# Cross-attention and FP8 feed-forward on one core: pair 2's statistics moved ahead, batch 0's residual moved into stage 1, weight casts regrouped

## The chip, the cores and the metric

One core of one Trainium2 chip runs the whole kernel in one launch. The metric is device time in microseconds (us), lower is better, as the median of the runs. Engines are PE (TensorE), DVE (VectorE), ACT (ScalarE), POOL (GpSimd) and SP, which here only issues DMAs.

## The reference

```python
x = x + xattn(layernorm(x), ctx, ctx, Wq, Wk, Wv, Wfc, bfc)   # 16 batches x 128 tokens x 512, fp32
#   q = x Wq.T (32 heads of 16); k, v = ctx Wk.T, ctx Wv.T (8 groups of 16, 4 heads share one)
#   softmax(q k.T / 4) v, then Wfc and its bias
x = x + ffn(layernorm(x))                # operands rounded to float8_e4m3
#   gelu(x Wg0) * (x Wg1), hidden 2048, then W_linear back to 512
```

## The kernel before, in words

The 16 batches go in 8 pairs (`NB = 2`). Stage p computes the attention of pair p in slots n = 0 to 18 (`SLOTS`; DVE has one more), and in the same slots prepares pair q = p + 1: its layer norm, keys (k), values (v), transposed x (x), queries (q) and the first score tiles for the row maxima. Behind the slots of stages 1 to 7 come units: a unit is a quarter of one batch's gate and ff products (32 matmuls of 128 columns), which ACT evicts (`gate_out`, `ff_out`) and DVE multiplies and rounds to fp8 (`product`, `act_fp8`). Stage 0 has no units, stage 1 has twelve (batches 0, 1 and 2), later ones eight. The second FFN product (`down`) lies in the slots of the next stage.

The order on each engine is written by hand: all five engine programs walk the same slots and units, and `PLAN_0`, `PLAN_1` and `PLAN` say in which slot a step lies. Engines run their own program in order and meet only at semaphores, so a step in a bad slot holds up all that stands behind it on its engine.

In a slot PE does `scores_t` (L618, the transposed scores of one head group), `weigh_values` (L639, L641) of the tile three slots back, and what the plan adds: `scores` (L587, for the maxima), `project_k`, `project_v` (L541), `turn_x` (L552), `project_q` and `project_out` (L506 to L508), `turn_out` (L655), `turn_x2` (L689). ACT exponentiates twice (`weights`: L921, L924), POOL forms the low part (`weights_lo`, L1412) that `weigh_values` needs, and DVE forms the maxima (`maxima`, L1182), the sums and quotients of the outputs (L1193, L1195, L1205) and the low parts of split fp32 operands (L1091, `keys_lo` L1157). The layer norm is `norm_stats` (L1112 to L1117, DVE), a power on POOL (`norm_rstd`, L1386), a copy of the root into a PSUM bank (`roots_1`, L1128) and `norm_apply_psum` (L1141, DVE). A batch's chain behind attention is `turn_out`, `out_hi`, `out_lo`, `project_out`, `residual` (L1219 to L1225), `norm2_rstd` (L1391), `roots_2`, `norm2_apply_psum` (L1241), `turn_x2`, `x2_out` (L936).

The FFN weights come as fp32 chunks of 128 x 1024 into staging places that are used in turn. POOL clamps a chunk (`chunk_clamp`, L1432), ACT casts it (`chunk_cast`, L862), and SP loads the next chunk for the place behind that cast; five chunks go over DVE instead (`chunk`, L1105). SP's queue also issues the DMAs that stack keys, queries and maxima (`mask_k`, `stack_k`, `stack_q`, `stack_max`) in one fixed order.

PSUM has eight banks, A, T, O and G with two each. `bank_sequence` writes down which product takes which bank, and a product waits for the reader of the one ahead of it in its bank. `exp_table` and `gelu_table` load ACT's function tables between attention and FFN.

Of the kernel before, what the change touches and what calls it, by code (L numbers as in the profile page):

```python
# [147 lines left out]
def bank_sequence():  # L148
# [6 lines left out]
    seq += [(("X", 1, 0), "A1"), (("X", 1, 1), "A0"), (("M", 0, 1), "G0"), (("Q", 1, 0), "A1"), (("Q", 1, 1), "A0")]  # L155
    seq += [(("S", 1, 0, s), name) for s, name in enumerate(("G0", "G0", "G0", "G0", "A1", "G0", "A1", "G0"))]
# [23 lines left out]
def xattn_ffn_kernel(nc, x_d, ctx_d, w_d, bfc_d, out_d):  # L180
    ctx = ExitStack()
    with ctx:
# [321 lines left out]
        def _(pe):  # L504
# [153 lines left out]
            def project_out(b, lo, hi):  # L658
                if lo == 0:
# [10 lines left out]
                    if chain_in_e(b) and b and b + 5 <= BATCHES:  # L670
# [109 lines left out]
            for p in range(NP):  # L780
# [3 lines left out]
                for n in range(SLOTS):  # L784
# [9 lines left out]
                    if p == 1 and n == X2_FIRST:  # L794
                        turn_x2(0)
# [25 lines left out]
                for k in range(len(units(p))):  # L821
# [14 lines left out]
                    if q < NP:  # L836
                        for s in BEHIND_UNIT.get(k, ()):
# [12 lines left out]
        def _(act):  # L850
# [168 lines left out]
            for p in range(NP):  # L1019
                q, plan = p + 1, PLANS[p]  # L1020
                chain, c_b = plan["chain"], max(0, NB * p - 1)
                for n in range(SLOTS):
# [8 lines left out]
                    if p == 1 and n == X2_FIRST:  # L1031
# [57 lines left out]
        def _(dve):  # L1089
# [47 lines left out]
            def norm_apply_psum(q, i):  # L1137
# [152 lines left out]
            keys_lo(1)  # L1290
            values_sum(1)
            late = list(W_DVE)
            for p in range(NP):
# [3 lines left out]
                for n in range(SLOTS + 1):  # L1297
# [47 lines left out]
                u0, c_b = units_through(p - 1), NB * p
                for k in range(len(units(p))):
# [190 lines left out]
```

## Time and profile before

| | |
|---|---|
| median of 3 runs | 446.52 us (445.78 to 449.13) |
| the profiled execution | 447.5 us, its span 445.7 us |
| granted PE clock, mean over the span | 0.988 of full speed |
| slots of stage 0 on PE | about 30.4 to 61.0 us |
| slots of stage 1 on PE | 61.0 to about 96.2 us |
| units of stage 1 on PE | about 96.2 to 125.0 us |

The profile is of one execution. Times of rows count from the start of its span, and the time outside the span is 447.5 - 445.7 = 1.8 us. Busy times are of one engine; the idle time of a row stands in brackets, with the instruction that ended it.

### The profile page before, as it was taken

The page shows a single profiled execution, that of the slowest core. Times are in us where ns is not written, and L with a number is a line of the kernel's source. Part 1 is how long each engine was busy: PE and PEld are TensorE (multiplying, and loading weights), DVE is VectorE, ACT ScalarE, POOL GpSimd, SP SyncE. Part 2 cuts the span into 40 slices and gives each one's busy share as a digit, 9 for nine tenths or more (in the row PEclk, how much of TensorE's full clock was granted, in tenths as well). Part 3 has the DMA queues.
Part 4 walks back from the last instruction along what each step waited for, and adds up shares of the span by engine and source line. Part 5 has one row for each costly group of instructions (what it writes and reads, how often), then busy time and mean ns, then how long its engine had stood idle before and what let it go on. Part 6 is the DMA issues. An engine that isn't in the chain of part 4 may idle for free.

```text
span 445.7 us, 11828 instructions
## 1 busy us (share of the span) xinstructions
PE 419.2 (94%) x4620; PEld 342.0 (77%) x4620; DVE 328.5 (74%) x705; ACT 313.4 (70%) x579; POOL 241.5 (54%) x232
## 2 busy tenths in 40 slices
PE   7868878989989999999999999999999999899997
PEld 7756556878866779877987789877887789657983
DVE  3786887588958578975997679975997679576442
ACT  6748849877897645888479755888479755895541
POOL 5388888966447613586228823686328823393000
PEclk9998998999999999999999999999999999999999
DMA  8887981568622551034701552034701342000001
GB/s 297 287 200 256 297 224 37 134 203 246 221 93 67 171 126 46 0 83 133 168 4 38 153 127 68 2 84 134 166 3 32 91 107 63 1 26 26 1 27 47
DMA packets 21287, 50.06 MB, mean 112 GB/s; under 512 B 4688, under 2 KB 5200, under 8 KB 21200
## 3 DMA queue, kind: packets, MB, share of 16 engines
q1 hardware_dynamic: 21054, 48.89, 38.5%
q8 instruction: 37, 0.61, 0.6%
q10 hardware_dynamic: 178, 0.41, 0.4%
q14 instruction: 18, 0.15, 0.1%
HBM read 23.86 MB, written 4.19 MB: 63 GB/s over the span
## 4 chain that ended last, share of the span: by engine, by line
PE 78%; DVE 11%; ACT 5%; issue 3%; DMA 1%; POOL 1%; DVEq 0%; POOLq 0%; ACTq 0%
PE bank L719 21%; PE bank L741 11%; PE bank L506 8%; PE bank L507 7%; PE bank L508 7%; PE bank L618 6%; PE bank L587 6%; DVE mneg L1182 4%; PE bank L639 3%; PE bank L641 3%; PE bank L541 2%; PE bank L552 2%; DMA qs<-mrow 1%; PE bank L655 1%; DVE prod L1247 1%
## 5 line engine op out<-in xcount | busy, mean ns | idle before, releaser
L1412 POOL TENSOR_TENSOR plo<-p,phi 128x512 f16<-128x512 f32 x128 | 148.4, 1170 | 57.1 <-ACT phi L924 56.1
L719 PEld LDWEIGHTS bank<-x2T,wgate 128*128 128x128 fp8e4 x2048 | 115.5, 98 | 11.6 <-issue 8.6
L719 PE MATMUL bank<-x2T,wgate 128*128 128x128 fp8e4 x2048 | 123.7, 219 | 0.8 <-DVE xr L1260 0.5
L921 ACT ACTIVATE p<-bank 128x512 f32<-128x512 f32 x128 | 77.6, 606 | 25.4 <-PE bank L618 24.5
L1182 DVE TENSOR_REDUCE mneg<-bank 128x4 fp32r<-128x512 f32 x128 | 83.9, 684 | 13.4 <-PE bank L587 13.4
L924 ACT ACTIVATE phi<-bank 128x512 f16<-128x512 f32 x128 | 77.3, 604 | 0.0
L741 PE MATMUL bank<-wlin,act 128*128 128x512 fp8e4 x256 | 70.8, 378 | 0.0
L943 ACT ACTIVATE gate<-bank 128x512 bf16<-128x512 f32 x64 | 38.3, 598 | 39.4 <-PE bank L719 38.2
L947 ACT CAST ff<-bank 128x512 bf16<-128x512 f32 x64 | 37.6, 587 | 34.5 <-PE bank L719 34.1
L618 PE MATMUL bank<-qs,ks 98*128 98x512 f32 x128 | 55.7, 435 | 4.3 <-DMA qs<-mrow 3.4
L587 PE MATMUL bank<-kmask,cq 128*128 128x512 f32 x128 | 51.6, 455 | 6.9 <-DVE mneg L1182 4.0
L639 PEld LDWEIGHTS bank<-vt,plo 128*128 128x128 f16 x512 | 31.9, 96 | 24.9 <-issue 21.3
L1391 POOL TENSOR_TENSOR rstd<-var,half_neg 128x1 f32<-128x1 f32 x16 | 8.8, 550 | 77.3 <-DVE var L1225 77.3
L639 PE MATMUL bank<-vt,plo 128*128 128x49 bf16 x512 | 44.8, 187 | 0.8 <-DVE ao L1205 0.8
L1247 DVE TENSOR_TENSOR prod<-gate,ff 128x512 bf16<-128x512 bf16 x64 | 33.7, 527 | 15.3 <-ACT ff L947 15.3
L641 PE MATMUL bank<-vt,phi 128*128 128x49 bf16 x512 | 43.0, 184 | 0.0
L506 PE MATMUL bank<-cx,wq 128*128 128x256 f32 x112 | 39.8, 355 | 1.5 <-DVE cx L1091 1.5
L1396 POOL TENSOR_TENSOR cx<-cin,cx 128x512 fp32r<-128x512 f32 x14 | 17.7, 1273 | 41.7 <-ACT cx L871 41.7
L1195 DVE TENSOR_REDUCE osum<-bank 128x128 f32<-128x384 f32 x64 | 35.7, 557 | 2.2
L1254 DVE TENSOR_SCALAR act<-prod 128x512 fp8e4<-128x512 bf16 x64 | 30.6, 478 | 2.9
L641 PEld LDWEIGHTS bank<-vt,phi 128*128 128x128 f16 x512 | 32.5, 97 | 0.1
L587 PEld LDWEIGHTS bank<-kmask,cq 128*128 128x128 f32 x128 | 22.8, 196 | 12.2 <-DVE mneg L1182 6.7
(112 smaller groups left out, 813.9 us busy)
## 6 DMA issues: line engine op xcount, KB each, us to landing
qs<-cq SPq DMA_DIRECT2D x93, 128.0 KB, 2.4
stage<-in_w SPq DMA_DIRECT2D x22, 512.0 KB, 4.7
ks<-khl SPq DMA_DIRECT2D x96, 64.0 KB, 2.0
cin<-in_ctx SPq DMA_DIRECT2D x8, 512.0 KB, 4.1
xr<-in_x SPq DMA_DIRECT2D x16, 256.0 KB, 4.3
out<-xr SPq DMA_DIRECT2D x16, 256.0 KB, 2.7
kmask<-khl SPq DMA_DIRECT2D x28, 64.0 KB, 2.0
raw<-in_w SPq DMA_DIRECT2D x3, 512.0 KB, 6.3
```

What stands on the lines that cost most here:

```text
L506: pe.matmul(out, a[1], b[0], start=first, stop=False)
L587: pe.matmul(bank_of("S", q, i, s)[:, :], cq[:, 0, j, tok(i)], kmask[:, 2 * half:2 * half + 2, :, tok(i)], start=True, stop=True).then_inc( ...
L618: pe.matmul(T[n % 2][:, :], ks[rows, p % 2, g // 2, g % 2, tok(i)], qs[rows, g // 2, :, tok(i)], start=True, stop=True).then_inc(st_done, 1)
L639: pe.matmul(out, plo[:, (TILES * p + n) % PBUF, j * SEQ:(j + 1) * SEQ], vt[:, p % 2, i, g, :], start=True, stop=False)
L641: mm = pe.matmul(out, phi[:, (TILES * p + n) % PBUF, j * SEQ:(j + 1) * SEQ], vt[:, p % 2, i, g, :], start=False, stop=True)
L719: mm = pe.matmul(out[:, h * SEQ:(h + 1) * SEQ], wgate8[:, UH * v + h, kk, part, :], x2T[:, b % ABUF, kk, :], start=kk == 0, stop=kk == KT - 1)
L741: mm = pe.matmul(lin_bank(b)[:, :], act8[:, b % ABUF, h, :], wlin8[:, h, :], start=h == 0, stop=h == HT - 1)
L921: act.activation(p32[:, e % P32BUF, :], T[n % 2][:, :], ACT.Exp, scale=QUARTER).then_inc(p32_ok, 1)
L924: act.activation(phi[:, e % PBUF, :], T[n % 2][:, :], ACT.Exp, scale=QUARTER).then_inc(phi_ok, 1)
L943: act.activation(gate[:, u % 2, :], up_bank[u % 2][0][:, :], ACT.Gelu_apprx_tanh).then_inc(gelu_ok, 1)
L1182: dve.tensor_reduce(dst[:, :, 2 * half:2 * half + 2, j].rearrange("p a r -> p r a"), bank_of("S", q, i, s)[:, :].rearrange("p (r a k) -> p ...
L1412: pool.tensor_tensor(plo[:, e % PBUF, :], p32[:, e % P32BUF, :], phi[:, e % PBUF, :], ALU.subtract).then_inc(plo_ok, 1)
```

## The change

Slots and units of stages 0 and 1 are rearranged; the arithmetic stays the same.

- `norm_stats(2)` and `norm_rstd(2)` move from slot 4 of stage 1 to the end of stage 0. Pair 2's roots are copied to bank G0 (last two columns) in slot 3, with no wait for `out_lo` any more, and its norm is applied in slot 4. `project_v` of pair 2 now waits for that norm.
- `residual(0)`, until now in slot 19 of stage 0 with the norm behind it, goes to slot 4 of stage 1, its norm to slot 6, `turn_x2(0)` from slot 3 to 7.
- In stage 1, v goes from slots 3, 4 to 5, 6, x from 7, 8 to 6, 7, q from 10 to 17 to 9 to 16, batch 1's chain from 4, 8 to 11, 12, 13, 15 to 8, 10 to 13, 14, 14, 16. `scores(2, 0, 3)` goes behind unit 0.
- `context_lo(2)` on POOL becomes `context_low(2)` on DVE, in slots 17 and 18 of stage 0. `keys_lo(1)` moves from ahead of stage 0 into its slot 5, and five score tiles of stage 0 and their banks change.
- The twelve casts of stage 1, one a unit before, are spread as `CAST_UNITS` says. The next context's high parts go from units 9, 10 to 5, 6, and the table load behind the last unit's `ff_out` goes ahead of it.

```diff
 CTX_SLOTS = (15, 16)
+CTX_UNITS = (5, 6)
+KEYS_SLOT = 5
+CAST_UNITS = {0: 1, 1: 3, 3: 1, 4: 1, 5: 1, 6: 1, 7: 1, 8: 1, 9: 1, 10: 1}
...
-              second={0: 2, 1: 1, 2: 1, 3: 2, 4: 2},
+              second={0: 2, 1: 2, 3: 1, 4: 2, 5: 1},
...
-              chain=dict(turn=13, project=(15, 16, 17, 18), residual=19, rstd=19, norm=19, turn2=None))
-PLAN_1 = dict(max=5, k=(0, 1), v=(3, 4), x=(7, 8), q=tuple(range(10, 18)), norm=4, even=17, next_max=None,
+              chain=dict(turn=13, project=(15, 16, 17, 18), residual=None, rstd=None, norm=SLOTS, turn2=None))
+PLAN_1 = dict(max=5, k=(0, 1), v=(5, 6), x=(6, 7), q=tuple(range(9, 17)), norm=2, even=17, next_max=None,
               second={0: 2, 1: 2, 2: 2, 3: 2},
-              early={16: 1, 17: 1, 18: 2}, m_early={17: 1, 18: 1},
-              chain=dict(turn=4, project=(8, 9, 10, 11), residual=12, rstd=12, norm=13, turn2=15))
+              early={16: 1, 17: 1, 18: 1}, m_early={17: 1, 18: 1},
+              chain=dict(turn=8, project=(10, 11, 12, 13), residual=14, rstd=14, norm=14, turn2=16))
...
-X2_FIRST = 3
+FIRST = dict(residual=4, rstd=4, norm=6, turn2=7)
+ROOT_AT = 2 * TOK - NB
...
+def behind(p, k):
+    return (3,) if p == 1 and k == 0 else BEHIND_UNIT.get(k, ())
...
-    seq += [(("X", 1, 0), "A1"), (("X", 1, 1), "A0"), (("M", 0, 1), "G0"), (("Q", 1, 0), "A1"), (("Q", 1, 1), "A0")]
-    seq += [(("S", 1, 0, s), name) for s, name in enumerate(("G0", "G0", "G0", "G0", "A1", "G0", "A1", "G0"))]
+    seq += [(("X", 1, 0), "A1"), (("X", 1, 1), "G1"), (("M", 0, 1), "G0"), (("Q", 1, 0), "A1"), (("Q", 1, 1), "A0")]
+    seq += [(("S", 1, 0, s), name) for s, name in enumerate(("G0", "G1", "G0", "G1", "A1", "G0", "A1", "G0"))]
...
+                    if q == 2:
+                        pe.wait_ge(xn_ok, NB * (q + 1))
...
-                    if q == NP - 1 and k == ups - 1:
+                    if q in (2, NP - 1) and k == ups - 1:
                         exp_table()
                     ff_out(u)
                     if p == 1:
-                        chunk_cast(clamped.pop(0))
+                        for _ in range(CAST_UNITS.get(k, 0)):
+                            chunk_cast(clamped.pop(0))
...
-            keys_lo(1)
             values_sum(1)
...
+                    if p == 1 and n == FIRST["residual"]:
+                        residual(0)
+                    if p == 1 and n == FIRST["norm"]:
+                        roots_2(0)
+                        norm2_apply_psum(0)
...
+                    if p == 0 and n - 2 in CTX_SLOTS:
+                        context_low(2, CTX_SLOTS.index(n - 2))
+                    if p == 0 and n == KEYS_SLOT:
+                        keys_lo(1)
...
+                if p == 0:
+                    norm_stats(2)
...
-                        if n == TILES:
-                            for h in range(2):
-                                context_lo(2, h)
```

## Rows read from the trace of the kernel before

**Rows 1.** The page's first part: busy time, share of span, instructions.

```profile
PE 419.2 (94%) x4620; PEld 342.0 (77%) x4620; DVE 328.5 (74%) x705; ACT 313.4 (70%) x579; POOL 241.5 (54%) x232
```

**Rows 2.** Busy time by stretch: stage 1's slots, its units, the boundary to stage 2.

```profile
core 0: us, PE busy (x) PEld busy (x) DVE busy (x) ACT busy (x) POOL busy (x), PEclk, DMA share, GB/s
61.00:96.18 35.18, 30.06 (x269) 23.89 (x270) 26.81 (x63) 27.38 (x52) 31.49 (x32) 0.90 0.46 140
96.18:125.03 28.85, 28.15 (x415) 25.87 (x414) 24.81 (x45) 22.54 (x36) 14.19 (x13) 1.00 0.78 224
125.03:135.29 10.26, 8.25 (x60) 5.95 (x58) 6.76 (x15) 9.86 (x18) 5.72 (x6) 1.00 0.12 44
```

**Rows 3.** The same view in stretches of 2 us, one of them, early in stage 1.

```profile
68.00:70.00 2.00, 2.00 (x6) 0.80 (x6) 1.96 (x4) 1.98 (x5) 1.98 (x3) 0.55 0.00 0
```

**Rows 4.** Timeline of PE, 44 to 96 us: start, length, line, [idle before <-releaser].

```profile
44.78 0.47 PE L587 MATMUL bank<-kmask,cq 128*128 128x512 f32 x1 [0.41 <-DMA kmask<-khl]
...
60.99 0.50 PE L618 MATMUL bank<-qs,ks 98*128 98x512 f32 x1 [0.20 <-DMA qs<-mrow]
...
65.06 1.10 PE L587 MATMUL bank<-kmask,cq 128*128 128x512 f32 x2 [2.15 <-DVE mneg L1182]
...
95.84 0.51 PE L587 MATMUL bank<-kmask,cq 128*128 128x512 f32 x1 [1.43 <-DVE cq L1091]
```

**Rows 5.** Timeline of the DMA queue on SP, around the end of stage 0.

```profile
58.62 0.67 SPq L425 DMA_DIRECT2D qs<-mrow  x1
```

**Rows 6.** Timeline of DVE, start of the kernel and stage 0 to stage 1.

```profile
7.52 0.69 DVE L1091 TENSOR_TENSOR wk<-raw,wk 128x512 fp32r<-128x512 f32 x1 [0.27 <-ACT wv L854]
...
60.90 0.69 DVE L1219 TENSOR_TENSOR xr<-xr,bank 128x512 f32<-128x512 f32 x1
...
64.32 2.57 DVE L1182 TENSOR_REDUCE mneg<-bank 128x4 fp32r<-128x512 f32 x4
...
69.24 0.87 DVE L1157 SCALAR_TENSOR_TENSOR khl<-bank,parity,khl 128x256 fp32r<-128x256 f32 x2
...
71.22 1.27 DVE L1112 BATCH_NORM_STATS2 bn<-xr 128x6 f32<-128x512 f32 x2
...
72.75 0.17 DVE L1117 TENSOR_SCALAR var<-mv 128x2 f32<-128x2 f32 x1
...
76.03 1.40 DVE L1141 SCALAR_TENSOR_TENSOR xn<-xr,mv,bank 128x512 f32<-128x512 f32 x2
```

**Rows 7.** Timeline of POOL, stage 0 to stage 1.

```profile
58.91 2.53 POOL L1396 TENSOR_TENSOR cx<-cin,cx 128x512 fp32r<-128x512 f32 x2
...
65.78 2.28 POOL L1412 TENSOR_TENSOR plo<-p,phi 128x512 f16<-128x512 f32 x2
```

**Rows 8.** Groups of POOL's instructions in stage 1's slots: xcount | busy, mean ns | idle.

```profile
L1412 POOL TENSOR_TENSOR plo<-p,phi 128x512 f16<-128x512 f32 x16 | 18.4, 1166 | 2.3 <-ACT phi L924 2.2
```

**Rows 9.** Timeline of ACT, units of stage 1 and the start of stage 2.

```profile
91.94 1.28 ACT L950 ACT_TABLE_LOAD   x1
...
103.75 1.06 ACT L862 ACTIVATE wgate<-stage 128x1024 fp8e4<-128x1024 f32 x1
...
107.09 0.62 ACT L936 ACTIVATE x2T<-bank 128x512 fp8e4<-128x512 f32 x1
...
127.17 1.12 ACT L862 ACTIVATE wlin<-stage 128x1024 fp8e4<-128x1024 f32 x1
128.31 1.28 ACT L953 ACT_TABLE_LOAD   x1
...
129.72 0.58 ACT L921 ACTIVATE p<-bank 128x512 f32<-128x512 f32 x1
```

**Rows 10.** Timeline of PE, units of stage 1 and the start of stage 2.

```profile
107.76 1.96 PE L719 MATMUL bank<-x2T,wgate 128*128 128x128 fp8e4 x32
...
127.75 0.39 PE L506 MATMUL bank<-cx,wk 128*128 128x256 f32 x1 [1.16 <-POOL cx L1396]
...
135.29 0.30 PE L596 MATMUL bank<-ident,mneg 128*128 128x128 f32 x1 [0.27 <-DVE khl L1157]
```

**Rows 11.** The products of gate and ff on DVE: min, median and max ns.

```profile
L1247 DVE TENSOR_TENSOR prod<-gate,ff x64: 407/416/1241, 98.9 to 436.3; 128x512 bf16<-128x512 bf16 x64
```

More of the change, by code:

```diff
@@ L669, in project_out @@
                     pe.wait_ge(aoT_lo, b + 1)
-                    if chain_in_e(b) and b and b + 5 <= BATCHES:
+                    if chain_in_e(b) and b > 1 and b + 5 <= BATCHES:
                         pe.wait_ge(xn_ok, b + 5)
@@ L793, in _ @@
                         turn_max(q, 0)
-                    if p == 1 and n == X2_FIRST:
+                    if p == 1 and n == FIRST["turn2"]:
                         turn_x2(0)
@@ L836, in _ @@
                     if q < NP:
-                        for s in BEHIND_UNIT.get(k, ()):
+                        for s in behind(p, k):
                             scores(q, *divmod(s, SBANKS))
@@ L1030, in _ @@
                         max_rows(q, 0)
-                    if p == 1 and n == X2_FIRST:
+                    if p == 1 and n == FIRST["turn2"]:
                         x2_out(0)
@@ L1079, in _ @@
                     if p == 1:
-                        chunk_cast(clamped.pop(0))
+                        for _ in range(CAST_UNITS.get(k, 0)):
+                            chunk_cast(clamped.pop(0))
                     if p == NP - 1 and k == 7:
                         x2_out(c_b + 1)
-                    if q + 1 < NP and k in (ups - 3, ups - 2):
-                        context_hi(q + 1, k - ups + 3)
-                if p and q < NP - 1:
+                    if q + 1 < NP and k in CTX_UNITS:
+                        context_hi(q + 1, CTX_UNITS.index(k))
+                if p > 1 and q < NP - 1:
                     exp_table()
@@ L1123, in root_2, with root_1 @@
                 return root(NB) if chain_in_e(b) else T[1][:, P:P + 1]
+            def root_1(q, i):
+                return G[0][:, ROOT_AT + i:ROOT_AT + i + 1] if q == 2 else root(i)
             def roots_1(q):
                 dve.wait_ge(rstd1_ok, q + 1)
-                dve.wait_ge(*((aoT_lo, NB * (q - 1)) if q >= 2 else (max_ok, 6)))
-                dve.tensor_copy(G[1][:, 0:NB], rstd1[:, :]).then_inc(root1_ok, 1)
+                if q != 2:
+                    dve.wait_ge(*((aoT_lo, NB * (q - 1)) if q > 2 else (max_ok, 6)))
+                dst = G[0][:, ROOT_AT:ROOT_AT + NB] if q == 2 else G[1][:, 0:NB]
+                dve.tensor_copy(dst, rstd1[:, :]).then_inc(root1_ok, 1)
             def roots_2(b):
@@ L1141, in norm_apply_psum @@
                 dve.scalar_tensor_tensor(xn[:, i, :], xr[:, (NB * q + i) % RING, :], mv1[:, i, 0:1],
-                                         root(i).broadcast_to([P, D]), ALU.subtract, ALU.mult).then_inc(xn_ok, 1)
+                                         root_1(q, i).broadcast_to([P, D]), ALU.subtract, ALU.mult).then_inc(xn_ok, 1)
             def norm_apply(q, i):
@@ L1322, in _ @@
                     if 1 < q < NP:
-                        if n == plan["norm"]:
+                        if q > 2 and n == plan["norm"]:
                             norm_stats(q)
@@ L1350, in _ @@
                     if q < NP:
-                        for s in BEHIND_UNIT.get(k - 1, ()):
+                        for s in behind(p, k - 1):
                             maxima(q, *divmod(s, SBANKS))
@@ L1372, in _ @@
                         finish(BATCHES - 3)
-                if q < NP and len(units(p)) - 1 in BEHIND_UNIT:
-                    for s in BEHIND_UNIT[len(units(p)) - 1]:
+                if q < NP:
+                    for s in behind(p, len(units(p)) - 1):
                         maxima(q, *divmod(s, SBANKS))
@@ L1471, in _ @@
                             values_low(1)
-                        if n == TILES:
-                            for h in range(2):
-                                context_lo(2, h)
                     elif q < NP:
-                        if n == plan["norm"]:
+                        if q > 2 and n == plan["norm"]:
                             norm_rstd(q)
@@ L1485, in _ @@
                         norm2_rstd(c_b)
+                    if p == 1 and n == FIRST["rstd"]:
+                        norm2_rstd(0)
                 if p == 1:
@@ L1490, in _ @@
                     norm2_rstd(NB * p)
+                else:
+                    norm_rstd(2)
                 if q < NP:
```

2 lines of the change are left out of this document (added).

## The prediction

> **What bounds the kernel now.** The page's first part comes first: PE is busy for 94% of the span, no other engine for more than 74% [rows 1]. Only two things can pay, then: time in which PE stands still, and time in which it runs at a lowered clock. I next cut the span where the change works and read busy time and granted clock there [rows 2]. Stage 1's slots take 35.18 us with 30.06 busy, 5.1 idle, at a mean clock of 0.90. Its units take 28.85 us with only 0.7 idle. The first 10.26 us of stage 2 hold 2.0 idle. A lowered clock is hidden in busy time: in one stretch of 2 us PE counts as 100% busy while the granted clock is 0.55, so it runs mostly at 1.2 instead of 2.4 GHz [rows 3]. A mean of 0.90 over 35.18 us costs 0.10 x 35.18 = 3.5 us. At full clock and without stalls PE would need 35.2 - 5.1 - 3.5 = 26.6 us for these slots, so 8.6 us lie there, and 2.0 at the start of stage 2. That is the stake.
>
> The timeline of PE names the stalls. Stage 1's slot 0 starts at 60.99, released by the DMA of the maxima. At 65.06 a score tile has waited 2.15 us for DVE's maxima, and at 95.84 one has waited 1.43 us for the low part of the queries [rows 4]. DVE's timeline says why the first is late: from 60.90 DVE does batch 0's residual, waits for POOL's power and applies the norm, and starts the maxima only at 64.32 [rows 6].
>
> **Part 1, stage 0.** Nothing in it shortens its end directly: slot 0 of stage 1 needs the DMA that SP issues at 58.62 [rows 5] and that lands 2.3 us later [rows 4], and SP gets there behind a row of stacking DMAs. The last score tile of pair 0 moves from slot 4 to 5, and `mask_k(1)`, which waits for it, follows. A slot is (60.99 - 44.78) / 13 = 1.25 us [rows 4]. The wait for the mask at 44.78 so grows by up to 1.25 us, against which DVE's queue is shorter by one tile ahead of pair 1's x (0.6 us) and `stack_max(0, 1)`, which follows the mask on SP, may go as early as before. Alternating banks for pair 1's maxima take short stalls away that SP's queue would have covered. I take 0 and keep -0.7 to +0.7.
>
> **Part 2, the boundary from stage 0 to 1.** From DVE's path go residual, wait, root and norm: 64.32 - 60.90 = 3.4 us, less the quotient of 0.3 that stays inside, so 3.1. There come the statistics of pair 2, 72.92 - 71.22 = 1.7 us, and two context low parts. The only row of that form alone is 0.69 us [rows 6], of which 0.6 counts back to back, so 1.2 together; most of it fits where DVE waited for PE's last tiles, and I take 0.3 (0 to 1.2). Net 3.1 - 1.7 - 0.3 = 1.1 us: maxima from about 63.2, and the stall of 2.15 us falls to about 1.0. POOL loses its two context steps at 58.91 (2.53 us), but that was time in which it waited anyway: it then waits for pair 2's variance until 63.1, does the power (0.7) and two bias additions (2.5), and begins the low weights at about 66.2 against 65.78 [rows 7].
>
> **Part 3, slots 0 to 5 of stage 1.** Here the change adds a wait. `project_v` of pair 2 stands at `xn_ok` for both norms, and DVE has ahead of them: eight maxima at 2.57 / 4 = 0.64 (5.0, a little overlapped), `keys_lo` 0.8, `residual(0)` with its statistics 1.8, two norms 1.4, a copy 0.2 [rows 6]. From 63.2 that is 9.2, so about 72.5. PE has little until then: six `scores_t`, eight scores, the keys, three `weigh_values`, 5.5 us of work in 11.5. Behind that wait on PE stand v, x, the queries and every later `scores_t`, and ACT and POOL behind those. Of 26.6 us PE has 26.6 - 5.5 = 21.1 left, less a score tile that moves out (0.2). So unit 0 starts at 72.5 + 20.9 = 93.4 at full clock. The second bound is POOL: 16 low weights at 1.14, the start to start of [rows 7, 8], are 18.3, four clamps 4.1, and small steps 2.4, so from 66.2 to 91.0. It idled 2.3 us of its time before [rows 8], so it is near its limit but not the last. Before, unit 0 started at 96.18. The gain is 2.8 at full clock. But PE now stands still for some 5 us in short pieces before 72.5, and before, 2.15 us of standing still at 62.9 to 65.06 was followed by the stretch at 0.55 [rows 3, 4]. One such stretch costs 0.9 us in 2, and may come or not: I take 0.6. The gain of the slots, part 2 and the stall of 1.43 us in it, is 2.2 us (0 to 4.9, the upper end by POOL's bound).
>
> On a smaller item: `turn_x2(1)` goes to slot 16, so ACT loads the gelu table (1.28, [rows 9]) ahead of `x2_out(1)`, for which `turn_out(2)` waits in slot 17. With ACT up to three tiles ahead of POOL this lies beside POOL's work. I count nothing; uncovered it is 1.3.
>
> TensorE's clock follows its own activity. The Trainium skill says the same (TensorE: Matmul & The Clock Gate, Part 1): half rate is the resting state and sustained activity releases it. The trace agrees [rows 3]. By that rule alone the scattered waits of part 3 should bring a low stretch back, and the slots' gain would be 1.9 instead of 2.2.
>
> **Part 4, the units.** PE was 28.15 of 28.85 us busy [rows 2], so nothing is to be won. Three casts now follow `ff_out(1)` in one go. ACT's old order from 103.75 was cast, gate, ff, cast, gate, `x2_out(2)` ending at 107.7, and unit 4, the first of batch 2, started at 107.76 [rows 9, 10]: that chain was already just in time. With one cast more in it, 0.95 us start to start, PE stalls 0.9 us, and the score tile behind unit 0 adds 0.2: a loss of 1.1 us (0.2 to 2). It doesn't spread, because unit 2 has no cast. Chunk loads are released earlier, never later, and POOL's clamps with them.
>
> **Part 5, the boundary from stage 1 to 2.** At the end ACT is last: cast of 1.12 at 127.17, table load of 1.28 at 128.31, the first exponential at 129.72 [rows 9]. The cast of unit 11 goes, the context steps leave units 9 and 10, and the load stands ahead of `ff_out(11)`. ACT then ends with `ff_out(11)` at about 127.4 and exponentiates 2.3 us earlier. The wait of 1.16 us for the context's low part at 127.75 goes too, as POOL has it ten us before. What is late next is DVE: statistics of pair 3 behind the product of unit 11, which are no earlier than before, POOL's power, a weight chunk, `keys_lo`, and then PE at 135.29 [rows 10]. POOL's power waited for POOL's first low weight, which is earlier by 2, so this path shortens by nearly 2 us. I take all of 10.26 - 8.25 = 2.0 (0.5 to 2.3).
>
> **The sum.** 0 + 2.2 - 1.1 + 2.0 = 3.1 us. The profiled execution took 447.5 (span 445.7 and 1.8 around it), 1.0 over the median, so it would give 444.4; from the median of 446.5 it is **443.4 us**. Later stages run the same programs and PE bounds them as well [rows 1], so I expect it to be kept.
>
> **The rivals.**
> - *POOL's pace.* If the maxima flow and no low clock comes, slots end by POOL's bound near 91.3: 4.9 instead of 2.2, so about 440.6. For it speaks the 3.5 us of clock loss that lie open, against it the nine us of DVE work ahead of `xn_ok`. Chance 0.22.
> - *The norm chain holds stage 2.* `ff_out(11)` comes after the load, so DVE's statistics of pair 3 start no earlier than 128.4, and if these set PE's step at 135.29, part 5 gives only 0.5: 444.9. Chance 0.14.
> - *Low parts on DVE wait for POOL.* The products of two SBUF operands on DVE take 0.416 us in the median and 1.241 at most [rows 11]. If the context low parts meet POOL's last low weights of stage 0, each waits up to one of 1.17 [rows 8], DVE is 1.1 later, and part 2 is gone: 444.5. Chance 0.10. The Trainium skill has this rule (SBUF — State Buffer, Who interferes with whom): a DVE instruction with two SBUF inputs and a GpSimd instruction that reads SBUF exclude each other. The spread of [rows 11] fits it, and it speaks against this move.
> - *Slower: the clock stays low in the dense slots.* The place is PE from the values of pair 2 on, where 20.9 us of work lie in one piece. Each us at 1.2 GHz there costs 0.5. If v, x and the first queries run low after the wait for `xn_ok`, 8 to 12 us of wall time, that is 4 to 6 us, and with the gain of 2.8 + 2.0 - 1.1 = 3.7 it turns at 7.5 us of low clock. At 12 us: 446.5 - 3.7 + 6 = 448.8, and more if the DMA queue of stage 0 is late too. Against it: before, such stretches lasted only some 3 to 4 us each. Chance 0.10.
> - The forecast itself, 441.5 to 445.3: 0.44.
>
> **The range.** It takes in the forecast, POOL's pace down to 440.2 and the slower case up to 448.0, with the unknown terms (stage 0 by 0.7, the units by 0.9): 440.2 to 448.0. One per cent, 4.5 us, is about what a measurement of this kernel can tell from no change. Below 442.05 lie POOL's pace (0.22) and a quarter of the forecast (0.11): 0.33. Above 451 lies the tail of the slower case: 0.06. The rest, 0.61, is within 1%.
>
> **What will show it.** The maxima of stage 1 start near 63.2 and the stall on them is about 1 us; `project_v` of pair 2 starts near 72.5, released by DVE's norm; unit 0 near 94 instead of 96.2; unit 4 shows a stall on ACT's x2T near 1 us; the first exponential of stage 2 comes about 2 us sooner behind the last unit. The prediction is wrong if the wait at `project_v` is short (POOL leads then), if the clock in the slots is above 0.97 or below 0.85, or if PE's idle time in the first 10 us of stage 2 stays at 2.

## The result, and the profile after

The changed kernel takes 450.3 us (median of 12 runs, 448.7 to 453.6) against 448.4 for the kernel before in the same rounds. The ratio is 1.0072 with a 95% interval of 1.0047 to 1.0098: by the ratio it is slower by 3.2 us, where 3.1 us less were forecast. The medians are only 1.9 us apart; the ratio compares means, 450.8 against 447.5, and leaves out one run of the kernel before that fell in a slower state. The profiled execution has a span of 448.6 us against 445.7.

Busy time and clock in the same three parts as in [rows 2], cut where they begin in the changed kernel: stage 1's slots, its units, the start of stage 2 up to `turn_max(2, 1)` (PE, its weight loads, DVE, ACT, POOL, then PE's granted clock):

```profile
core 0: us, PE busy (x) PEld busy (x) DVE busy (x) ACT busy (x) POOL busy (x), PEclk, DMA share, GB/s
60.04:96.94 36.90, 30.39 (x269) 23.96 (x269) 24.82 (x60) 27.84 (x52) 30.44 (x30) 0.91 0.44 133
96.94:127.07 30.13, 28.70 (x415) 25.96 (x415) 27.19 (x49) 23.31 (x37) 16.18 (x15) 1.00 0.78 228
127.07:136.69 9.62, 7.97 (x60) 6.01 (x58) 6.45 (x15) 8.72 (x17) 4.47 (x4) 1.00 0.02 5
```

The slots of stage 1 take 36.90 us instead of 35.18, with 30.39 us of busy PE instead of 30.06 and a mean clock of 0.91 instead of 0.90 [rows 2]: idle time grew from 5.1 to 6.5 us, and almost nothing of the clock came back. Shorter stretches show where the clock is low now, and a second place far behind the change:

```profile
70.00:74.00 4.00, 2.64 (x18) 2.26 (x19) 2.75 (x8) 1.82 (x5) 4.00 (x5) 0.56 0.05 12
74.00:78.00 4.00, 4.00 (x36) 3.76 (x36) 1.77 (x5) 3.14 (x6) 1.86 (x2) 0.59 0.44 107
78.00:82.00 4.00, 3.20 (x35) 2.45 (x35) 2.54 (x6) 4.00 (x10) 2.99 (x3) 1.00 0.36 85
386.00:390.00 4.00, 3.10 (x16) 2.22 (x17) 0.84 (x2) 2.91 (x7) 2.95 (x3) 0.74 0.00 0
390.00:394.00 4.00, 4.00 (x34) 2.69 (x31) 1.78 (x4) 3.05 (x7) 2.61 (x3) 0.84 0.01 4
```

For the kernel before, the same view has these rows:

```profile
66.00:70.00 4.00, 4.00 (x15) 2.61 (x14) 2.85 (x6) 2.79 (x6) 3.98 (x4) 0.57 0.40 161
...
74.00:78.00 4.00, 2.56 (x23) 1.76 (x22) 3.83 (x10) 4.00 (x9) 4.00 (x5) 0.83 0.12 29
78.00:82.00 4.00, 4.00 (x33) 3.07 (x33) 2.68 (x7) 3.41 (x9) 4.00 (x6) 0.74 0.45 109
...
386.00:390.00 4.00, 4.00 (x33) 2.78 (x33) 0.77 (x2) 3.52 (x8) 3.81 (x4) 1.00 0.00 0
390.00:394.00 4.00, 4.00 (x47) 2.10 (x46) 3.46 (x10) 3.83 (x9) 3.95 (x5) 1.00 0.01 4
```

The kernel before has two low stretches in stage 1's slots, at 66 to 70 us and within 74 to 82 us. The changed kernel has one, at 70 to 78 us, where it does the values, transposes and weighing of stage 1. Its loss in the two rows is 0.44 x 4 + 0.41 x 4 = 3.4 us, and before it was 0.43 x 4 + 0.17 x 4 + 0.26 x 4 = 3.4 us as well: in this pair of profiles the loss didn't grow, it failed to go away. At 386 to 394 us another 0.26 x 4 + 0.16 x 4 = 1.7 us are lost, in code that the change doesn't touch. The profile of the kernel before has a stretch like that in stage 0 instead (clock 0.95 from 28 to 60 us, 1.00 in the changed kernel), so both profiles lose about 5.1 us in all. Only the means over many runs, below, differ.

PE's timeline, with the stalls of the changed kernel (L628 is `scores_t`, L597 `scores`, L649 `weigh_values`, L551 `project_v`, L667 `turn_out`, L701 `turn_x2`, L731 `up`, L606 `turn_max`):

```profile
60.04 0.50 PE L628 MATMUL bank<-qs,ks 98*128 98x512 f32 x1
...
62.82 1.10 PE L597 MATMUL bank<-kmask,cq 128*128 128x512 f32 x2 [0.86 <-DVE mneg L1200]
...
69.94 0.18 PE L649 MATMUL bank<-vt,plo 128*128 128x49 bf16 x1 [1.16 <-POOL plo L1440]
...
71.66 2.05 PE L551 MATMUL bank<-wv,cx 128*128 128x256 f32 x8 [1.36 <-DVE xn L1159]
...
79.38 0.66 PE L667 MATMUL bank<-ident,ao 128*128 128x128 f32 x4 [0.68 <-ACT x2T L948]
...
94.30 0.38 PE L701 MATMUL bank<-ident,xn 128*128 128x128 fp8e4 x4 [1.18 <-DVE xn L1259]
...
95.37 0.65 PE L667 MATMUL bank<-ident,ao 128*128 128x128 f32 x4 [0.40 <-ACT x2T L948]
...
96.94 1.07 PE L731 MATMUL bank<-x2T,wgate 128*128 128x128 fp8e4 x16
98.56 0.66 PE L731 MATMUL bank<-x2T,wgate 128*128 128x128 fp8e4 x9 [0.55 <-DVE aoT L1104]
...
110.50 1.68 PE L731 MATMUL bank<-x2T,wgate 128*128 128x128 fp8e4 x27 [0.85 <-ACT x2T L948]
...
127.07 0.48 PE L628 MATMUL bank<-qs,ks 98*128 98x512 f32 x1
...
131.82 0.47 PE L628 MATMUL bank<-qs,ks 98*128 98x512 f32 x1 [0.89 <-ACT phi L936]
...
136.69 0.30 PE L606 MATMUL bank<-ident,mneg 128*128 128x128 f32 x1 [0.77 <-DVE khl L1175]
```

From these rows follow the ledger against the kernel before, the time at which both reach the same step:

| step on PE | before | after | difference |
|---|---|---|---|
| slot 0 of stage 1 | 60.99 | 60.04 | -0.95 |
| unit 0, gate half | 96.18 | 96.94 | +0.76 |
| unit 4 | 107.76 | 110.50 | +2.74 |
| slot 0 of stage 2 | 125.03 | 127.07 | +2.04 |
| `turn_max(2, 1)` | 135.29 | 136.69 | +1.40 |
| end of the span | 445.7 | 448.6 | +2.9 |

The 1.4 us stay to the start of stage 7; there the 1.5 us at 386 to 394 come in. DVE's, POOL's and ACT's timelines show what releases these steps (DVE: L1200 maxima, L1237 `residual`, L1159 the norm of pair 2, L1259 that of batch 1, L1125 `norm_stats`; POOL: L1440 the low weights, L1419 batch 1's root; ACT: the table loads, L948 `x2_out`, L959 `ff_out`, L933 the first exponential):

```profile
62.07 2.58 DVE L1200 TENSOR_REDUCE mneg<-bank 128x4 fp32r<-128x512 f32 x4
...
68.37 0.68 DVE L1237 TENSOR_TENSOR xr<-xr,bank 128x512 f32<-128x512 f32 x1
...
70.11 1.41 DVE L1159 SCALAR_TENSOR_TENSOR xn<-xr,mv,bank 128x512 f32<-128x512 f32 x2
...
93.41 0.75 DVE L1259 SCALAR_TENSOR_TENSOR xn<-xr,mv,bank 128x512 fp8e4<-128x512 f32 x1
...
131.60 1.28 DVE L1125 BATCH_NORM_STATS2 bn<-xr 128x6 f32<-128x512 f32 x2
```

```profile
90.30 2.29 POOL L1440 TENSOR_TENSOR plo<-p,phi 128x512 f16<-128x512 f32 x2 [0.38 <-ACT phi L936]
92.55 0.56 POOL L1419 TENSOR_TENSOR rstd<-var,half_neg 128x1 f32<-128x1 f32 x1
```

```profile
92.25 1.28 ACT L962 ACT_TABLE_LOAD   x1
...
94.72 0.60 ACT L948 ACTIVATE x2T<-bank 128x512 fp8e4<-128x512 f32 x1 [0.98 <-PE bank L701]
...
128.72 1.28 ACT L965 ACT_TABLE_LOAD   x1
...
130.12 0.57 ACT L959 CAST ff<-bank 128x512 bf16<-128x512 f32 x1
130.59 0.60 ACT L933 ACTIVATE p<-bank 128x512 f32<-128x512 f32 x1
```

### The profile page after: what moved, and what is told of

Its sections match the earlier page's. It is cut to its first block, busy times and chain, and to the rows that moved or that the text cites. A ratio compares the mean times of both kernels' runs of the same rounds, so it can differ in the third digit from the quotient of the medians.

```text
span 448.6 us, 11828 instructions
## 1 busy us (share of the span) xinstructions
PE 419.0 (93%) x4620; PEld 340.7 (76%) x4620; DVE 328.9 (73%) x707; ACT 313.5 (70%) x579; POOL 239.3 (53%) x230
## 4 chain that ended last, share of the span: by engine, by line
PE 73%; DVE 13%; ACT 6%; issue 4%; POOL 2%; DMA 1%; ACTq 0%; DVEq 0%; POOLq 0%
PE bank L731 21%; PE bank L753 11%; PE bank L514 7%; PE bank L515 6%; PE bank L516 6%; PE bank L628 5%; PE bank L597 5%; DVE mneg L1200 5%; PE bank L649 3%; PE bank L551 3%; PE bank L651 2%; DMA qs<-mrow 1%; PE bank L562 1%; PE bank L667 1%; DVE osum L1213 1%
## 5 line engine op out<-in xcount | busy, mean ns | idle before, releaser
L1440 POOL TENSOR_TENSOR plo<-p,phi 128x512 f16<-128x512 f32 x128 | 148.2, 1167 | 65.9 <-ACT phi L936 65.0
L731 PE MATMUL bank<-x2T,wgate 128*128 128x128 fp8e4 x2048 | 124.0, 219 | 2.2 <-ACT x2T L948 0.9
L731 PEld LDWEIGHTS bank<-x2T,wgate 128*128 128x128 fp8e4 x2048 | 115.6, 98 | 13.5 <-issue 9.8
L933 ACT ACTIVATE p<-bank 128x512 f32<-128x512 f32 x128 | 77.8, 608 | 27.9 <-PE bank L628 27.2
L1200 DVE TENSOR_REDUCE mneg<-bank 128x4 fp32r<-128x512 f32 x128 | 84.0, 685 | 12.2 <-PE bank L597 12.2
L959 ACT CAST ff<-bank 128x512 bf16<-128x512 f32 x64 | 37.5, 587 | 35.3 <-PE bank L731 35.0
L628 PE MATMUL bank<-qs,ks 98*128 98x512 f32 x128 | 55.1, 431 | 3.4 <-DMA qs<-mrow 2.4
L597 PE MATMUL bank<-kmask,cq 128*128 128x512 f32 x128 | 50.9, 446 | 4.3 <-DVE mneg L1200 2.3
L649 PEld LDWEIGHTS bank<-vt,plo 128*128 128x128 f16 x512 | 32.0, 96 | 26.8 <-issue 23.0
L1419 POOL TENSOR_TENSOR rstd<-var,half_neg 128x1 f32<-128x1 f32 x16 | 8.8, 547 | 76.3 <-DVE var L1243 76.3
L649 PE MATMUL bank<-vt,plo 128*128 128x49 bf16 x512 | 44.9, 188 | 2.2 <-POOL plo L1440 1.4
L1424 POOL TENSOR_TENSOR cx<-cin,cx 128x512 fp32r<-128x512 f32 x12 | 15.4, 1288 | 35.7 <-ACT cx L883 35.7
L1272 DVE TENSOR_SCALAR act<-prod 128x512 fp8e4<-128x512 bf16 x64 | 31.6, 494 | 2.9
L514 PE MATMUL bank<-wfc,aoT 128*128 128x512 f32 x64 | 29.8, 466 | 2.0 <-DVE aoT L1104 1.9
```

Source lines behind the costliest of these rows:

```text
L514: pe.matmul(out, a[1], b[0], start=first, stop=False)
L597: pe.matmul(bank_of("S", q, i, s)[:, :], cq[:, 0, j, tok(i)], kmask[:, 2 * half:2 * half + 2, :, tok(i)], start=True, stop=True).then_inc( ...
L628: pe.matmul(T[n % 2][:, :], ks[rows, p % 2, g // 2, g % 2, tok(i)], qs[rows, g // 2, :, tok(i)], start=True, stop=True).then_inc(st_done, 1)
L649: pe.matmul(out, plo[:, (TILES * p + n) % PBUF, j * SEQ:(j + 1) * SEQ], vt[:, p % 2, i, g, :], start=True, stop=False)
L731: mm = pe.matmul(out[:, h * SEQ:(h + 1) * SEQ], wgate8[:, UH * v + h, kk, part, :], x2T[:, b % ABUF, kk, :], start=kk == 0, stop=kk == KT - 1)
L933: act.activation(p32[:, e % P32BUF, :], T[n % 2][:, :], ACT.Exp, scale=QUARTER).then_inc(p32_ok, 1)
```

## The experiments

Each kernel ran up to 12 times beside the kernel before on the same chip. e8 to e11 ran on another chip than e1 to e7, so across these groups the ratios compare better than the spans. Every run lists its span and mean granted clock, so a mean can be split: (1 - clock) x span is what the low clock costs at most, and the rest is work and waits at full clock. The split is an estimate, and it gives too much to the clock, since PE also stands still in part of the low time: among the runs of one kernel, all kernels of the table taken together, the span grows by about 0.56 us for each us of that loss. A difference in the clock column is so worth a little over half of itself in time, and what is over belongs to the last column.

| kernel | runs | ratio to before (95%) | mean span | mean clock | lost to the clock | rest |
|---|---|---|---|---|---|---|
| before, beside e1 to e4 | 22 | | 445.1 | 0.9922 | 3.5 | 441.6 |
| before, beside e5 to e7 | 31 | | 445.8 | 0.9899 | 4.5 | 441.2 |
| before, beside e8 to e11 | 27 | | 445.2 | 0.9907 | 4.1 | 441.0 |
| after | 12 | 1.0072 (1.0047 to 1.0098) | 449.0 | 0.9866 | 6.0 | 442.9 |
| after, again | 12 | 1.0078 (1.0051 to 1.0105) | 449.3 | 0.9860 | 6.3 | 443.0 |
| e1, units part only | 12 | 1.0001 (0.9976 to 1.0025) | 445.0 | 0.9900 | 4.5 | 440.5 |
| e2, slots part only | 6 | 1.0099 (1.0065 to 1.0132) | 449.1 | 0.9860 | 6.3 | 442.8 |
| e3, residual(0) in slot 5 | 12 | 1.0053 (1.0028 to 1.0078) | 447.2 | 0.9905 | 4.3 | 443.0 |
| e4, batch 1's chain earlier | 6 | 1.0114 (1.0075 to 1.0152) | 449.5 | 0.9878 | 5.5 | 444.0 |
| e5, three casts in unit 0 | 9 | 1.0088 (1.0058 to 1.0119) | 449.8 | 0.9860 | 6.3 | 443.5 |
| e6, projection joined | 12 | 1.0066 (1.0037 to 1.0094) | 448.6 | 0.9874 | 5.7 | 443.0 |
| e7, waits filled | 12 | 1.0055 (1.0028 to 1.0083) | 448.1 | 0.9905 | 4.3 | 443.8 |
| e8, before + units + S(2,0,3) | 7 | 0.9955 (0.9935 to 0.9975) | 442.8 | 0.9923 | 3.4 | 439.4 |
| e9, before, waits filled | 12 | 1.0005 (0.9987 to 1.0023) | 445.0 | 0.9944 | 2.5 | 442.5 |
| e10, e8 + e9 | 9 | 0.9950 (0.9929 to 0.9970) | 442.8 | 0.9947 | 2.4 | 440.5 |
| e11, norm of pair 2 in slot 3 | 12 | 1.0023 (1.0006 to 1.0041) | 446.3 | 0.9917 | 3.7 | 442.6 |

Single runs of one kernel spread by about 1 us (standard deviation) in the last column, so a mean of 12 is known to about 0.3, and two such means can differ by some 0.8 by chance.

**The changed kernel again.** Unchanged, as the yardstick.

> The changed kernel once more, as the yardstick on the same chip. Of its distance to the kernel before, about 1.3 us should be there at full clock (the shift that the trace shows at the start of stage 3) and the rest in the mean granted clock, 0.986 to 0.988 against 0.992. Rival (the clock is chance, the same for all): the same mean clock as before and a distance of 1.3.

Against the kernel before beside it the span is 3.5 us longer: 1.8 are clock (6.3 against 4.5), 1.8 the rest. The rival, a clock by chance alone, falls: two sets of 12 runs have 0.9866 and 0.9860, three sets of the kernel before 0.9899 to 0.9922. The means don't say in which stage the extra loss lies.

**e1 and e2, the two halves.** e1 puts only the units part on the kernel before; e2 takes it out of the changed kernel:

```diff
-                    if q in (2, NP - 1) and k == ups - 1:
+                    if q == NP - 1 and k == ups - 1:
...
-                        for _ in range(CAST_UNITS.get(k, 0)):
-                            chunk_cast(clamped.pop(0))
+                        chunk_cast(clamped.pop(0))
...
-                    if q + 1 < NP and k in CTX_UNITS:
+                    if q + 1 < NP and k in (ups - 3, ups - 2):
```

> The kernel before with only the units part of the change: casts grouped as 1, 3, 0, 1, ..., the context's high parts in units 5 and 6, the table load ahead of the last unit's ff_out. Slots theory (the loss sits in stage 1's slots, the units are about neutral: minus 0.9 for the late x2T of batch 2, plus 0.6 to 1.4 at the start of stage 2): within 0.5 us of the kernel before, stall of about 0.9 us at unit 4. Rival, the units part carries the loss: 1.5 to 3 us slower than before. Rival, my forecast of part 5: 1 us faster than before.

> The changed kernel with the units part undone (one cast a unit, context in units 9 and 10, table load last). Slots theory: still 2 to 3.5 us slower than the kernel before; low clock after the wait of project_v for pair 2's norm, turn_x2(1) waits 1.2 us. Rival, units part carries the loss: equal to before or up to 1 us faster.

The loss is in the slots part, which here means all but the units, stage 0 too: e2 keeps it in full, e1 is level with before. In e1 the x2T stall at unit 4 is there as forecast, and so is DVE's `keys_lo` as the last thing at the start of stage 2 (view of PE's waits: total, times, longest):

```profile
PE bank L721 <- ACT x2T L938: 0.8, 1, 0.8
...
PE bank L598 <- DVE khl L1160: 0.8, 1, 0.8
```

**e3, batch 0's residual behind pair 2's norm.**

```diff
-FIRST = dict(residual=4, rstd=4, norm=6, turn2=7)
+FIRST = dict(residual=5, rstd=5, norm=6, turn2=7)
```

> The changed kernel with batch 0's residual in slot 5 of stage 1, behind pair 2's norm, instead of slot 4 ahead of it. Theory (the values of pair 2 wait for DVE, PE stands still and its clock falls): project_v starts 1.3 to 1.8 us sooner, near 70 us, the clock in 70 to 78 us is higher or low for less time, and the whole is 1.5 to 4 us faster than the changed kernel. Rival (the end of the slots is set by batch 1's chain, early time is given back there): project_v sooner but the whole within 0.7 us of the changed kernel. Rival (the clock falls anyway, since PE has little work there): the low stretch stays 6 to 7 us long and the whole gains under 1.5.

`project_v` no longer waits for the norm, and the loss to the clock falls from 6.0 to 4.3, while the rest stays at 443.0: the time is given back at `turn_x2(0)`, whose chain is now late. In e3's view of PE's waits, 61 to 137 us, `turn_x2` has this row:

```profile
PE bank L701 <- DVE xn L1259: 3.6, 2, 2.4
```

So both sides hold in part: without the wait less is lost to the clock, and as a wait it only changes its place. In e3's profile the clock is 1.00 in all slots of stage 1, although PE stands still for 2.40 us in one piece at `turn_x2(0)`. A wait of that length need not bring a low stretch.

**e4 and e6, batch 1's chain earlier.** e4 has `project=(9, 10, 11, 12), residual=13, rstd=13, norm=13, turn2=15`, e6 this:

```diff
-              chain=dict(turn=8, project=(10, 11, 12, 13), residual=14, rstd=14, norm=14, turn2=16))
+              chain=dict(turn=8, project=(10, 11, 12, 12), residual=13, rstd=13, norm=13, turn2=15))
```

> The changed kernel with batch 1's output projection in slots 9 to 12, residual in 13, its norm behind it and turn_x2(1) in slot 15 ahead of the gelu table load, instead of each one slot later. Theory (this chain is late by 2 us at the end of the slots: 1.2 for turn_x2(1), 0.4 for turn_out(2), 0.5 for the gate product): these three waits go and unit 0's second half starts 1.5 to 2.1 us sooner, whole 1.5 to 2 us faster than the changed kernel. Rival (PE's work or POOL's low weights hold the same place): under 0.5 us.

> The changed kernel with the last two quarters of batch 1's projection together in slot 12, its residual in 13 and turn_x2(1) in slot 15; the first quarter stays in slot 10, where the kernel of e4 (9 to 12) stood 1.4 us. Theory (the late chain costs 1.2 + 0.4 + 0.5 at the end of the slots): unit 0's second half starts 1.3 to 2 us earlier than 98.6, whole 1.3 to 2 faster. Rival (the wait for out_lo(2), which needs the last slot's quotients and queries on DVE, takes the place): under 0.5 us.

Neither gains in the last column (444.0 and 443.0 against 442.9 and 443.0, with 6 runs of e4). In e4 the projection in slot 9 stands until `out_lo(1)` is there. In e6 PE's waits from 90 to 105 us are 0.8 and 1.3 instead of 1.2, 0.4 and 0.6: the second half of unit 0 now waits for `out_lo(2)`. The rival holds in e6: at the end of the slots several steps are late together. The view of e6's waits:

```profile
PE bank L731 <- DVE aoT L1104: 1.3, 1, 1.3
PE bank L701 <- DVE xn L1259: 0.8, 1, 0.8
```

**e5, the three casts in unit 0.**

```diff
-CAST_UNITS = {0: 1, 1: 3, 3: 1, 4: 1, 5: 1, 6: 1, 7: 1, 8: 1, 9: 1, 10: 1}
+CAST_UNITS = {0: 3, 1: 1, 3: 1, 4: 1, 5: 1, 6: 1, 7: 1, 8: 1, 9: 1, 10: 1}
```

> The changed kernel with the casts of units 0 and 1 exchanged, 3 in unit 0 and 1 in unit 1; ACT stands idle after unit 1's gate. Theory (three casts ahead of x2_out(2) hold unit 4 by 0.85 us): no stall on x2T at unit 4 and 0.8 to 1.0 us faster than the changed kernel. Rival (the wait moves to DVE, whose maxima and products follow): stall gone, whole the same within 0.4.

The stall on x2T at unit 4 is gone and the time isn't less (443.5 against 443.0). PE waits for the maxima more, 3.0 us in four places against 1.2 in two. Two of the four, 0.62 and 0.77 us, are new and lie in the units. The price of 0.85 us that I had put on the casts is a stall that shows, but not time that could be had back by this edit. The row in e5's view of waits:

```profile
PE bank L597 <- DVE mneg L1200: 3.0, 4, 1.3
```

**e7, PE's waits filled.** Ten matmuls that nobody reads, four in slot 4 and six in slot 5 of stage 1:

```diff
+            def fill(count):
+                for _ in range(count):
+                    pe.matmul(O[1][:, 400:512], ident[:, :], ident[:, 0:112], start=True, stop=True)
...
+                    if p == 1 and n in (4, 5):
+                        fill((0, 0, 0, 0, 4, 6)[n])
```

> The changed kernel with ten more matmuls of 112 columns whose result nobody reads (about 1.9 us of PE), four in slot 4 and six in slot 5 of stage 1, where PE waits 1.16 us for the low weights and 1.36 us for pair 2's norm. Clock theory (PE's idle time there brings the low clock for the values, transposes and first queries): the stretch 70 to 78 us stays near full clock, ST(1, 7) comes 2 to 3 us sooner and the whole is 1.5 to 3 us faster than the changed kernel although it does more. Rival (the clock falls from the thin load of the weigh_values slots, or by chance): no change or up to 0.5 us slower.

The stretch is at full clock from 70 to 78 us, against 0.56 and 0.59 in the changed kernel (busy time by stretch, as above):

```profile
70.00:74.00 4.00, 3.25 (x36) 2.64 (x36) 3.90 (x9) 3.02 (x7) 4.00 (x5) 1.00 0.13 52
74.00:78.00 4.00, 4.00 (x45) 3.62 (x45) 2.19 (x6) 2.71 (x7) 4.00 (x5) 1.00 0.13 31
```

Over 12 runs the loss to the clock falls by 2.0 us, from 6.3 to 4.3, and the rest grows by 0.8, as the filler costs more than the waits had room for. The kernel does more and is 1.2 us faster than the changed one in mean span, less than the 1.5 to 3 expected; the intervals of the ratios overlap (1.0055 against 1.0078). The clock column, not the total, carries the finding.

**e9 and e10, the same on the kernel before.** Ten fillers where it waits 2.15 us, in slot 1, and four in slot 6:

```diff
+                    if p == 1:
+                        if n == 1:
+                            pe.wait_ge(ao_ok, SUMS * p - 1)
+                            fill(O[0], 10)
+                        if n == 6:
+                            fill(O[1], 4)
```

> The kernel before with fourteen unread matmuls of 112 columns (2.6 us of PE), ten where PE waits 2.15 us for the maxima in slot 1 of stage 1 and four in slot 6. Clock theory (the low stretches of the kernel before too come from standing still there): clock of 66 to 82 us near 1.00 instead of 0.5 to 0.85, mean clock up by 0.004 to 0.008, 1.5 to 3 us faster than the kernel before. Rival (it comes from the thin load of the weigh_values slots or from before slot 1): same clock and up to 1 us slower.

> e8 and e9 together. If their gains add: 3 to 5 us faster than the kernel before, ratio 0.989 to 0.994. If filling gains nothing: equal to e8 or up to 1 us slower.

The low stretches of stage 1 vanish here too, in the same view of e9 (0.57 and 0.83 in these rows of the kernel before):

```profile
66.00:70.00 4.00, 3.67 (x30) 2.50 (x29) 3.73 (x8) 3.43 (x8) 4.00 (x5) 1.00 0.42 170
...
74.00:78.00 4.00, 3.24 (x39) 2.36 (x35) 3.13 (x8) 3.37 (x8) 4.00 (x5) 1.00 0.28 68
```

The mean clock rises to 0.9944, and 1.6 us of clock loss go, but 1.5 us of other time come in: no gain in all, against what I expected. e10 doesn't beat e8 either. So unread work in PE's waits is enough to end the low clock behind them, and it pays nothing. Filling takes about as much from the clock loss of the kernel before (1.6 us) as of the changed one (2.0), and what is left is 2.5 against 4.3. So the extra clock loss of the changed kernel isn't shown to lie in stage 1's slots.

**e8, the kernel before with the units part and one score tile behind unit 0.** Stage 0 and all other slots as before:

```diff
-              early={16: 1, 17: 1, 18: 2}, m_early={17: 1, 18: 1},
+              early={16: 1, 17: 1, 18: 1}, m_early={17: 1, 18: 1},
...
+def behind(p, k):
+    return (3,) if p == 1 and k == 0 else BEHIND_UNIT.get(k, ())
```

> The kernel before with the units part and scores(2, 0, 3) behind unit 0 instead of in slot 18, stage 1's other slots and stage 0 as before. Theory (these are the parts of the change that pay; the wait of 1.43 us at 95.84 goes and 0.23 of work moves): unit 0 starts 1.2 us sooner after the start of the slots than in the kernel before, whole 1.5 to 2.5 us faster than the kernel before at full clock, ratio 0.994 to 0.998. Rival (unit 0's gate product then waits for out_lo(2), as in the changed kernel): under 1 us.

0.9955 (0.9935 to 0.9975): 2.4 us less in mean span than the kernel before. Of this 1.7 is in the last column, which with 7 runs that spread by 1.7 is known only to about 0.7. The ratio is clear of 1. This version beats both kernels, and it is the change without its slots. As e1, the units part alone, is level with before, the score tile seems to make the difference, alone or together with the units. No kernel had the tile alone.

**e11, pair 2's norm one slot earlier.**

```diff
-PLAN_1 = dict(max=5, k=(0, 1), v=(5, 6), x=(6, 7), q=tuple(range(9, 17)), norm=2, even=17, next_max=None,
+PLAN_1 = dict(max=5, k=(0, 1), v=(5, 6), x=(6, 7), q=tuple(range(9, 17)), norm=1, even=17, next_max=None,
```

> The changed kernel with pair 2's norm applied in slot 3 of stage 1, one slot earlier and ahead of batch 0's residual, which stays in slot 4. Theory (project_v waits for DVE, 1.4 us at 71.7, the new wait of the change): the wait on xn at project_v goes, ST(1, 6) comes 1 to 1.5 us sooner relative to the start of the slots, turn_x2(0) waits less than the 2.4 us of the kernel with the residual in slot 5, and the slots as a whole take 1 to 3 us less. Rival (POOL's low weights and the thin load remain, the clock falls all the same): full-clock time within 0.5 us of the changed kernel and the same loss of clock.

This number alone takes 2.7 us off the changed kernel's mean span (446.3 against 449.0) and the ratio from 1.0072 to 1.0023, which is 2.2 us. The clock loss falls by 2.3 us (3.7 against 6.0), the rest by 0.4. The wait for the norm is gone from the view of PE's waits; POOL's low weights and the end of the slots are still in it:

```profile
PE bank L649 <- POOL plo L1440: 1.3, 2, 1.1
PE bank L701 <- DVE xn L1259: 1.2, 1, 1.2
PE bank L667 <- ACT x2T L948: 1.2, 2, 0.8
```

## Why the prediction was wrong

**The stake.** That 3.5 us of clock and 5 us of stalls lay in the slots was right, though by the 0.56 above such a loss is worth some 2 us and not 3.5. The error was to let the change start from 26.6 us at full clock and pay back only what I listed.

**Part 1, stage 0,** 0 with 0.7 either way: slot 0 of stage 1 began at 60.04, 0.95 before its time in the kernel before. This is luck of the pair: stage 0 of the kernel before has a low stretch in its profile and that of the changed kernel has none. The kept profiles can be compared by the clock from 28 to 60 us:

| clock, 28 to 60 us | start of stage 1's slot 0, stage 0 as before | with the new stage 0 |
|---|---|---|
| 1.00 | no profile | 60.04 (after), 60.86 (e4) |
| 0.95 | 60.33 (e10), 60.99 (before), 61.05 (e9) | 61.43 (e6), 61.45 (e3), 61.94 (e11), 61.97 (again), 62.80 (e2) |
| 0.89 | no profile | 63.22 (e5), 63.83 (e7) |
| 0.84 | 62.71 (e8), 62.81 (e1) | no profile |

At 0.95 the means are 60.8 and 61.9. So the new stage 0 ends about 1.1 us later, an estimate from eight profiles, and more than the 0.7 that I allowed. No kernel had it alone.

**Part 2, the boundary.** Right. Maxima start at 62.07 in a trace that is 0.95 ahead there, for 63.2 forecast; the stall of 2.15 became 0.86, for about 1.0. The rival of the port between DVE and POOL falls: the two context low parts took 1.29 us together and POOL stood still beside them, having ended its last low weight of stage 0 at 58.05, before DVE began at 58.21. So no run here tests the lock that the Trainium skill describes (SBUF — State Buffer, Who interferes with whom) on these two steps; it just had nothing to hit.

**Part 3, the slots. This is the step that failed.** The new wait came as worked out: `project_v` at 71.66, released by DVE's norm, for 72.5 forecast. Two terms behind it were mis-sized. From `project_v` to unit 0 the kernel takes 96.94 - 71.66 = 25.3 us, where I had 20.9.

- *"One such stretch costs 0.9 us in 2, and may come or not: I take 0.6."* The low clock came and lasted some 7 us, and PE had its dense work in it: 3.4 us in this profile, of which 2.8 lie behind `project_v`. As the kernel before loses the same 3.4 in its slots, nothing of what I had coming back came back. In the mean of its runs the changed kernel loses 6.0 to 6.3 us to the clock, against 3.5 to 4.5 before. e11, e3 and e7 bring the loss down in three ways, by ending the wait or by filling it, to 3.7, 4.3 and 4.3. That filling alone does it is what the Trainium skill would say (TensorE: Matmul & The Clock Gate, Part 1: activity releases the throttle), and e7 and e9 agree with 1.00 in stretches that were at 0.56 to 0.83. I had the mechanism as the slower rival, with 7.5 us of low clock as the point from which it decides, and gave it 0.10 because each stretch before was short. The two of them together were as long as the one is now, and that sum was the number to carry over. Nor did the rival's own sum fit: at some 7 us of low clock it gives no loss at all, so the clock alone doesn't explain the miss. Its case of 12 us, 448.8, lay outside my range as well, which ended at 448.0.
- *"So unit 0 starts at 72.5 + 20.9 = 93.4 at full clock."* This puts every wait behind `project_v` at nothing, without a reason. `turn_out(1)` waited 0.68 us at 79.38 for `x2_out(0)`, `turn_x2(1)` 1.18 us for batch 1's norm (93.41 on DVE, whose root POOL makes only behind its low weights, at 92.55), then `turn_out(2)` 0.40 for `x2_out(1)`: 2.3 us before unit 0. The second half of unit 0 waited another 0.55 for `out_lo(2)`. Of these only `turn_out(2)`, with the gelu table ahead of it, was on my list, as *"I count nothing; uncovered it is 1.3"*, and there I was right: the load is over at 93.74 with its small ACTIVATE, and `x2_out(1)` then waits 0.98 for PE's `turn_x2(1)`. I had taken 2.8 us of gain from PE's remaining work alone, and didn't walk batch 1's chain, moved by one to four slots, through its engines. e4 and e6 show that moving it one slot earlier gains nothing.

**Part 4, the units,** a loss of 1.1: the stall at unit 4 measured 0.85, for 0.9 worked out, and the kernel lost 2.04 - 0.76 = 1.3 us from unit 0 to stage 2, the 0.55 just named in it. Right, with e5's warning that the stall isn't worth its length.

**Part 5, the start of stage 2,** a gain of 2.0: it gave 2.04 - 1.40 = 0.64. The rival with 0.5 us was nearly the true case. The first exponential comes 3.52 us after slot 0 instead of 4.69. But `ff_out(11)` stands behind the table load, so DVE's statistics of pair 3 start at 131.60, 4.53 after slot 0, where it was 3.33, and PE waits 0.77 for `keys_lo` behind them. PE's idle time in this part is 9.62 - 7.97 = 1.65 us, for 2.0 before. My worry, that these statistics *"are no earlier than before"*, was right and too small: they are later.

**The sum.** Forecast 0 - 2.2 + 1.1 - 2.0 = -3.1 us. In the profiled pair, from slot 0 of stage 1 on: +1.7 to unit 0, +1.3 in the units, -0.6 at stage 2, less the 0.95 by which slot 0 was early, 1.4 in all; and 1.5 of low clock in stage 7. In the means of runs: 1.3 to 1.8 in the rest and 1.8 to 2.6 of clock; at 0.56 us for each us of clock loss this is 1.0 to 1.4 us for the clock and some 2.5 for waits and work.

What the runs show of the 3.2 us is this: e11, which moves one step by one slot, takes 2.2 of them back, so most of the loss hangs on the new wait. What e11 still has over the kernel before, 1.0 us by its ratio, is about what the estimate for stage 0 gives. The waits at the end of the slots are the other candidate, and no run removed them together or undid stage 0 alone, so this part stays open.

Whether the low clock in stage 7 belongs to the change is open too: it is in the profiles of the changed kernel, its repetition, e3, e7 and e11, and not in those of before, e1, e2, e4, e5, e6, e8, e9 and e10. All fourteen profiles have the same wait ahead of it, 1.75 us for `out_lo` at 382 to 391 us.

## What to carry to other kernels

A stall on PE has two prices, its length and the low clock that may follow, and the second is paid by the work that comes next. So when a change moves a wait, ask what PE does in the microseconds behind it. And add up all low stretches of the kernel before, not the longest one. A step whose result three engines pass on should be walked through all of them at its new place before any gain is counted, and a gain taken from "PE's work left" is only an upper bound. Test the parts of a bundle alone: here the units with one score tile were worth 0.45%, and the rest cost more than that.

## What the runs showed of the hardware

The granted clock differs from run to run of one kernel, 0.981 to 1.000 in the 12 runs of e1, and the span follows: 442.6 us at 1.000, 443.6 at 0.996, 446.8 at 0.981. In the profiles the differences lie in stretches of some 3 to 4 us at half clock (0.50 from 72 to 76 us of the changed kernel), or of two or three times that, each single one worth 1.7 us in the clock column. In time it costs about half: from 1.000 to 0.981 are 8.5 us of clock loss and 4.2 us of span, so 0.8 us for each of five.

The same wait isn't always followed by a low stretch. The 1.75 us in stage 7 are in all fourteen profiles, and the clock falls behind them in five; 2.40 us in e3 were followed by none. One profile of each kernel can therefore not rank two schedules, nor size one stage, but the mean clock and the span of a dozen runs can rank them, and profiles sorted by their low stretches can size a stage.
